# First expert layer (layer 1) computed on tokens sorted by expert: indexed transfers, 40 blocks of 256 rows, weights copied from a register address

## The reference

```python
h = rmsnorm(x, g1); c = h @ w_down
... causal attention with 16 heads of 4 on c ...
x = x + o @ w_up
t = rmsnorm(x, g2).reshape(-1, D)                  # 4096 tokens, D = 128
probs = softmax(t @ router_w)                      # E = 8 experts
vals, idx = top_k(probs, 2);  w = vals / sum(vals)
gate = sum(one_hot(idx, E) * w)                    # two entries per token
hid = silu(einsum('td,edf->tef', t, w1)) * einsum('td,edf->tef', t, w3)   # F = 256
y = einsum('tef,efd->ted', hid, w2)
return res + einsum('ted,te->td', y, gate)
```

## Time and profile before

| | |
|---|---|
| median of three runs | 2375.21 us |
| the profiled execution, its time | 2380.9 us |
| its span, first to last instruction | 2379.1 us |
| mean granted TensorE clock | 0.902 |
| PE busy | 2093.7 us (88%) |
| DVE busy | 1531.5 us (64%) |
| ACT busy | 1066.7 us (45%) |
| POOL busy | 606.8 us (26%) |

### The profile page before, as it was taken

One profiled execution on the slowest core, in us unless ns is written; L12 is line 12 of the kernel. 1 busy time (PEld: TensorE's weight loads), 2 busy tenths in 40 slices (PEclk: granted clock), 3 DMA queues, 4 the chain that ended last, 5 costly groups with the idle time before them and its releaser, 6 DMA issues. The chain is left out here.

```text
span 2379.1 us, 40889 instructions
## 1 busy us (share of the span) xinstructions
PE 2093.7 (88%) x15206; PEld 1293.5 (54%) x15206; DVE 1531.5 (64%) x4178; ACT 1066.7 (45%) x1905; POOL 606.8 (26%) x867
## 2 busy tenths in 40 slices
PE   3688889998588888799999999988899999999993
PEld 1455556676476666455654556544554555555552
DVE  5677665432577776577747766557855677776655
ACT  2344533332355556244543434424354556555542
POOL 3421002001422221232202322243301233433232
PEclk9888889999789999799999999985569999999995
DMA  7556300300455554121200200016520000000001
GB/s 191 108 124 125 65 1 15 57 1 1 82 93 104 105 103 111 36 53 42 57 16 1 45 1 1 1 60 142 128 57 25 10 10 10 9 10 10 10 1 36
DMA packets 153138, 121.94 MB, mean 51 GB/s; under 512 B 21980, under 2 KB 145828, under 8 KB 147236
## 3 DMA queue, kind: packets, MB, share of 16 engines
q1 hardware_dynamic: 152940, 119.32, 23.0%
HBM read 78.04 MB, written 39.85 MB: 50 GB/s over the span
## 5 line engine op out<-in xcount | busy, mean ns | idle before, releaser
L1841 DVE TENSOR_REDUCE mneg<-psb 128x4 f32<-128x512 f32 (+1 forms) x576 | 388.7, 685 | 168.4 <-PE psb L1441 165.8
L2139 ACT ACTIVATE HB<-psb 128x512 f32<-128x512 f32 x384 | 226.7, 598 | 203.7 <-PE psb L1441 200.7
L1441 PE MATMUL psb<-K,Q 96*128 96x128 bf16 x1280 | 192.4, 256 | 54.7 <-DVE mneg L1841 32.7
L1440 PE MATMUL psb<-HB,KS 128*128 128x512 f32 x512 | 232.9, 598 | 0.0
L1441 PE MATMUL psb<-Q,K 99*128 99x128 bf16 x1280 | 150.3, 251 | 79.6 <-DMA Q<-mT 79.4
L1982 DVE TENSOR_TENSOR OE<-psb,OE 128x512 f32<-128x512 f32 x120 | 82.7, 689 | 191.1 <-ACT OE L2211 190.4
L2321 POOL TENSOR_SCALAR rs<-mv 128x2 f32<-128x2 f32 (+1 forms) x104 | 24.0, 230 | 712.0 <-DVE mv L1799 704.0
L2211 ACT ACTIVATE OE<-psb 128x512 f32<-128x512 f32 x128 | 76.5, 597 | 287.6 <-PE psb L1440 287.3
L2139 ACT ACTIVATE HB<-psb,bias 128x512 f32<-128x512 f32 x192 | 131.9, 687 | 145.4 <-PE psb L1441 143.8
L2207 ACT ACTIVATE HB<-psb,cols 128x512 f32<-128x512 f32 x256 | 171.3, 690 | 44.5 <-PE psb L1440 43.2
L1441 PEld LDWEIGHTS psb<-K,Q 96*128 96x128 bf16 x1280 | 112.1, 113 | 132.3 <-issue 61.5
(11 more groups left out here) (347 smaller groups left out, 4637.4 us busy)
## 6 DMA issues: line engine op xcount, KB each, us to landing
K<-sc_k SPq DMA_DIRECT2D x32, 384.0 KB, 5.0
Q<-sc_q SPq DMA_DIRECT2D x32, 384.0 KB
sc_q<-comp SPq DMA_DIRECT2D x48, 192.0 KB, 2.3
sc_q<-comp SPq DMA_DIRECT2D x48, 128.0 KB, 2.1
vraw<-in_ctx SPq DMA_DIRECT2D x48, 128.0 KB, 6.9
KS<-sc_s SPq DMA_DIRECT2D x16, 384.0 KB
K<-sc_k SPq DMA_DIRECT2D x32, 192.0 KB, 3.6
Q<-sc_q SPq DMA_DIRECT2D x32, 192.0 KB, 4.4
```

What stands on the lines that cost most here:

```text
L1440: return pe.e.matmul(out, w, x, start=start, stop=stop)
L1441: return pe.e.matmul(out, w, x, start=start, stop=stop, skip_group_check=True)
L1841: t = e.tensor_reduce(m.mneg[:, s.b % 4, s.i * A.per:(s.i + 1) * A.per], PSB[s.use.bank].rearrange("p (h k) -> p h k", h=A.per), AX.X, ALU ...
L2139: a.done(act(m.HB[:, s.slot, :], PSB[s.use.bank], ACT.Exp, bias=bz), s.use.drained)
```

## The change

The first expert layer no longer sends all tokens through all experts. Each of the 8192 pairs of a token and one of its two experts gets a row of a table in DRAM, sorted by expert; 40 blocks of 256 rows are then computed, each by one expert, and each token fetches its two results.

- All eight fronts (sorted_front) now stand in run_f1, started after every fourth b. gate_rank is followed by gate_pick (12 DVE instructions, for gate_top's 9: masks and weights of the first and second expert) and place: PE counts with small bf16 matmuls how many tokens of each expert stand before each token, and DVE makes row numbers of it (five instructions).
- scatter: POOL writes the normalized tokens to tok_rows by indirect transfers, eight of 128 rows per group, 64 in all. 
- The weights w1 and w3 are split into high and low parts in run_f1 (8 times halves of 128x512), not in the expert stage.
- block_table: after the last front, 24 small DVE instructions write for each block where its rows start and where its expert's weights stand, into an SBUF table. SP writes zero rows behind each expert's last row (pad_rows, 16 transfers, eight of them at an address read from the table).
- expert_blocks: for each of 40 blocks SP loads 256 rows from an address in the table; PE turns them; ACT copies them out of PSUM; DVE splits them; ACT and DVE copy the high and low parts of the expert's weights, 128x512 each, from an address in a register to a fixed buffer; PE computes 12 f32r matmuls of 256 columns and 4 f32 matmuls of 128x128; ACT, DVE: silu and product; DVE copies the result out of PSUM; SP stores it to y_rows. The number of blocks is fixed. Each address is read by the engine itself from the table (value_load): 40 times each on PE, DVE and ACT, 48 times on SP.
- gather and combine: for each b POOL fetches the two result rows of each token (two indirect transfers), and DVE adds them with their weights to U and X. Four b come before the preparations of layer 2's attention, eight among these, and 20 in its main loop, one per b.
- load2, and with it every preparation of layer 2's attention, is now started behind the blocks.

```diff
     def end_f1(b, k, u):
...
-        if b in (3, 7):
-            front1(b // 4, ("vraw", 0), "big_r")
+        if b % 4 == 3:
+            front1(b // 4)
...
+    def expert_blocks(t_m, w_done):
...
+        for n in range(NBLK + 2):
+            if n == 4:
+                do("y_index", need=(tuple(scattered), start), done=t_idx)
+            for j in ([0, 1] if n == 0 else [n + 1]):
+                if j < NBLK:
+                    do("block_load", j=j, need=(ready, start), free=t_full.get(j - 3))
...
+            if n < NBLK:
+                j = n
...
+                do("block_turn", j=j, use=u, need=(loaded[j], start), raw_free=split_done.get(j - 2), free=up_full.get(j - 2), done=split_done[j])
...
+                do("block_weights", j=j, need=(t_tab, t_m, w_done, start), free=up_full.get(j - 2), hi=w_ready[j][0], lo=w_ready[j][1])
+            if 0 <= n - 1 < NBLK:
+                j = n - 1
...
+                do("block_up", j=j, ua=ua, ub=ub, need=(split_done[j], w_ready[j]), at_free=h_done.get(j - 2), h_free=(down_full.get(j - 8), start))
...
+            if 0 <= n - 2 < NBLK:
+                j = n - 2
...
+                do("block_down", j=j, use=u, need=h_done[j], free=stored.get(j - 3))
+                down_full[j] = u.full
+                do("block_store", j=j, need=u.drained)
...
+    chain([(lambda i=i: split_weights(i), 10) for i in range(8)], 10)
     run_f1()
...
-    moe(5, up1, None, each1, lambda g: load2() if g == 0 else None)
...
+    y_stored, blocks_done = expert_blocks(t_m, tuple(w_done))
+    after_blocks = now()
+    for b in range(4):
+        gather(b, y_stored, blocks_done)
+    load2()
+    chain([lambda b=b: gather(b, y_stored, blocks_done) for b in range(4, 12)], 2)
+
+    def more(t):
...
+        if t + 12 < B:
+            gather(t + 12, y_stored, blocks_done)
...
     def block_up(s):                                   (PE)
...
+        for u, at_ in ((s.ua, 0), (s.ub, 256)):
+            pe.wait_ge(u.before)
+            o = PSB[u.bank]
+            for c in range(2):
+                w = slice(at_ + 128 * c, at_ + 128 * c + 128)
+                oc = o[:, 256 * c:256 * c + 256]
+                matmul(oc, m.whi[k][:, w], x[0], c == 0, False, False)
+                matmul(oc, m.whi[k][:, w], x[1], False, False, False)
+                t = matmul(oc, m.wlo[k][:, w], x[0], False, c == 1, False)
...
     def block_weights(s):                              (DVE; the same on ACT with whi and CFr)
+        v.wait_ge(s.need, s.free)
+        at_ = e.value_load(m.tab[0:1, 1, s.j:s.j + 1], min_val=0, max_val=4096 - 512)
+        v.done(e.tensor_copy(m.wlo[s.j % 2], m.WBr[:, bass.ds(at_, 512)]), s.lo)
...
     def gather(s):                                     (POOL)
+        g.wait_ge(s.need, s.free)
+        for k in range(2):
+            e.indirect_dma_start(m.gy[s.k][:, 128 * k:128 * k + 128], None, m.y_rows,
+                                 bass.IndirectOffsetOnAxis(ap=m.pidx[:, k, s.b:s.b + 1], axis=0)).then_inc(g.sems[f"dma_gy{s.k}"], 16)
...
     def block_load(s):                                 (SP; rows_of reads the address)
+        sp.wait_ge(s.need, s.free)
+        load(f"xs{s.j % 3}", m.xs[s.j % 3].rearrange("p (i d) -> p i d", i=2), rows_of(m.tok_rows, (0, s.j)).rearrange("(p i) d -> p i d", i=2))
```

More of the change, by code:

```diff
@@ L1080, in make_plan, with split_weights @@
     do("moe1_load", need=pe_after_ffn0)
-    t_m = dma("dma_moe1", 3)
+    t_m = dma("dma_moe1", 2)
     w_f[0] = now()
+    w_done = []
+    def split_weights(i):
+        w_done[:] = [halves(("CFr", 512 * i), ("WBr", 512 * i), ("WB", 512 * i), t_m, w_f[0])]
+    chain([(lambda i=i: split_weights(i), 10) for i in range(8)], 10)
     run_f1()
[L1084 to L1119, removed]
@@ L1121, in make_plan @@
-    moe(5, up1, None, each1, lambda g: load2() if g == 0 else None)
-    do("moe2_load", need=now())
+    while side:
+        slot_no[0] += 1
+        run_side(1)
+    y_stored, blocks_done = expert_blocks(t_m, tuple(w_done))
[5 more added lines that the diff above has]
+    def more(t):
+        if t == 0:
+            while 11 not in gathered():
+                slot_no[0] += 1
+                run_side(1)
+        if t + 12 < B:
+            gather(t + 12, y_stored, blocks_done)
@@ L1125, in make_plan, with gathered @@
+    def gathered():
+        return [s.b for s in P.steps if s.kind == "gather"]
+    do("moe2_load", need=after_blocks)
     t_w2, t_w1a = dma("dma_w2"), dma("dma_w1a")
-    do("k8_ones", need=P.last["pe"])
+    do("k8_ones", need=after_blocks)
     k8_free[0:4] = [inc("pool", "clear_pool")] * 4
@@ L1609, in gate_rows, with place @@
         pe.done(t, s.use.full)
[L1611 to L1622, removed]
-            pe.done(product(PSB[s.ub.bank], (m.KFr[:, o2:o2 + 128], m.WBr[:, o2:o2 + 128]), x), s.ub.full)
+    def place(s):
+        o = PSB[s.use.bank]
+        o3 = o[:, 0:32].rearrange("p (b e) -> p b e", b=4)
+        pe.wait_ge(s.need, s.use.before)
+        matmul(o[:, 0:32], m.trib[:, :], m.pickb[:, :, :].rearrange("p b e -> p (b e)"), True, False, False)
+        for j in range(3):
+            matmul(o3[:, j + 1:4, :], m.onesq[:, :], m.pickb[:, j:j + 1, :].broadcast_to([128, 3 - j, 8]), False, False, False)
+        for j in range(4):
+            t = matmul(o[:, 32:40], m.onesq[:, :], m.pickb[:, j, :], False, j == 3, False)
+        pe.done(t, s.use.full)
@@ new lines, in block_turn, with block_up @@
+    def block_turn(s):
+        turn(s.use, m.xs[s.j % 3], 2, s.need, C("ident"))
+    def block_up(s):
+        k = s.j % 2
+        x = m.xhi[k], m.xlo[k]
+        pe.wait_ge(s.need)
+        for u, at_ in ((s.ua, 0), (s.ub, 256)):
[7 more added lines that the diff above has]
+                t = matmul(oc, m.wlo[k][:, w], x[0], False, c == 1, False)
+            pe.done(t, u.full)
@@ new lines, in block_down @@
+    def block_down(s):
+        o, h = PSB[s.use.bank], m.HB[:, s.j % 8, :]
+        at_ = pe.e.value_load(m.tab[0:1, 2, s.j:s.j + 1], min_val=0, max_val=2048 - 256)
+        pe.wait_ge(s.need, s.use.before)
+        for i in range(2):
+            for c in range(2):
+                t = matmul(o[:, 128 * i:128 * i + 128], h[:, 256 * c + 128 * i:256 * c + 128 * i + 128],
+                           m.WB[:, bass.ds(at_ + (4096 + 128 * c), 128)], i == 0 and c == 0, c == 1, False)
+        pe.done(t, s.use.full)
```

277 lines of the change are left out of this document (250 added, 27 removed).

## The result

| | before | after |
|---|---|---|
| median of the first runs (five each) | 2375.21 us | 2392.35 us |
| profiled execution, time and span | 2380.9, 2379.1 us | 2381.07, 2379.3 us |
| run_f1, to the last addition to U | 1237 | 1283 |
| from there to the first turn of a block (called the gap) | - | 38 us |
| expert stage; its blocks | 353 us | 140 us |

The ratio of the runs is 1.0056, 95% interval 1.0029 to 1.0084: slower by 0.6%, 17 us between the medians, where 51 were forecast. The stages of the two profiled executions, which this document compares, sum to no difference (-353 + 46 + 38 + 140 + 130, and -1 behind them): that of the changed kernel lies 11 us under its median, that of the kernel before 5.7 over it.

What follows compares the result with a forecast made beforehand. The prediction took PE to bound the 353 us expert stage. It summed -353 + 51 + 45 + 252 + 32 + 24 = +51 onto 2380.9 us, took off 5.7, and forecast 2426 us, range 2395 to 2485 us.

Steps and rivals of the forecast that it cites:

- wrong in the main: The prediction's own test: blocks starting less than 4.8 us apart, or run_f1 not growing.
- forecast 252 us: Expert blocks: 42 x 6.0 us, taking half the blocks at the circle's pace and half at a lower PE clock.
- The circle through SP: Blocks: load of block n+2 waits behind store of n-2; 5.2 plus 5.0 us per two blocks, at least 5.1 each.
- the clock's share of 0.9: Blocks: half run with PE at 1.2 GHz, 6.7 us instead of 5.1, giving near 6.0 us a block.
- my first rival: Blocks: readings cost an instruction's pace, clock holds; about 3.9 us a block, 164 us, 2338 us in all; chance 0.25.
- forecast +32 and +24: Layer 2's attention: +32 us at its start, no longer covered; +24 in its main loop, 1.2 us per b.
- The third rival: Indirect transfers cost POOL the upper bound, 2.1 us, delaying attention and run_f1's splits; 2494 us; chance 0.17.
- forecast +51: run_f1: fronts 2 to 5 31 us, pick and place 10, weight halves 10; 30 to 80 us possible.
- The halves: run_f1: eight splits of 128x512 expert weights into high and low parts on DVE, forecast at 10 us.
- forecast +45: Between run_f1 and the blocks, PE idle: front 7, table instructions, zero-row transfers and the first block's rows.
- Front 7: The last front, starting with the last b and covered by nothing: 18 us (12 to 25) ahead of the blocks.
- my range: The forecast's own range, 2395 to 2485 us: blocks of 5.3 to 6.9 us, the rest 20 us either way.

Runs made afterwards that it cites:

- early_load: Changed kernel with the rows of block n+2 loaded one block earlier, ahead of the store that waits for DVE: 2364.81 us, 0.9932 of the kernel before.
- reads_x5: Changed kernel with each table reading in the blocks on SP and DVE done five times over: 2481.33 us, 1.0433 of the kernel before.
- defer: Changed kernel with each combination two attention steps (in the start two fetches) behind its fetch: 2313.69 us, 0.9706 of the kernel before.
- scatter_apart: Changed kernel with each front's eight indirect stores in four pairs, five slots apart, not one burst: 2380.71 us, 1.001 of the kernel before.
- two edits more: Added to deferral and early loads: new order at the start of layer 2's attention, weight halves behind the block table: 2296.65 us, 0.9648 of the kernel before.

## Why the prediction was wrong

The sign was right, the size was not, and the nearness of the sum is luck: it hides two larger errors that cancel. The forecast named a sign of being wrong in the main, blocks that start less than 4.8 us apart, and they did, at 3.4 in the mean.

- **The blocks: forecast 252 us, measured 140.** This is the step that failed. The circle through SP is there, as forecast: early_load breaks it, and reads_x5 lengthens it by what it adds. Its links were mis-sized. From DVE's copy to PE's turn I had 5.2 us and the trace has 3.2, from the turn to the next copy 5.0 and 3.4. A reading's load takes 0.27 to 0.31 us and the whole reading 0.55 to 0.62, not 1.28 with 0.4 for the registers; I had taken it from a table load on ACT, a different thing. And the sum counted an issue twice: the landing of a load runs from the start of its issue, and PE turns 0.04 us behind it, 2.04 us in all where I had 0.6 + 2.4 + 0.4. I had also let PE's clock fall to 1.2 GHz in half of the blocks, on rows of the start of layer 2's attention, where PE had been idle first; it stayed at 1.00 from 1335 us on. Of the 6.0 us a block, the circle was 1.7 too long and the clock's share of 0.9 did not come. This was my first rival, which gave a block 3.9 us and 164 in all (its own 5.1 - 1.1 is 4.0, a slip of 4 us over the stage): right in its mechanism, and still too slow. The Trainium skill (DMA: Bandwidth & Descriptors, section Latency and other measured facts) gives a floor of about 600 ns; the trace disagrees, since 263 ns is the least of 48.
- **Layer 2's attention: forecast +32 and +24, measured +130.** I had the price of an indirect transfer right (1.2 us taken, 1.25 measured) and saw that DVE would stand if POOL was not ahead, 4.8 us at a time. I then took 1.2 us per b, a quarter of that, by DVE's idle time before. It is the other way round: DVE feeds POOL, so POOL can't be ahead of a DVE that waits. 116 us of waits, 73 of which defer gave back. The start is dearer than forecast too: with the waits gone, defer's stage is still 57 us longer than before, where 32 stood. The third rival named this sign, "DVE's combination waiting for POOL's transfers", with the wrong cause: it needed no dearer transfer. POOL's 64 fetches took 940 to 1124 ns in after, with a median of 956, so what the Trainium skill (SBUF — State Buffer, section SBUF: two separate sides) warns of can have held none of them by more than 0.2 us.
- **run_f1: forecast +51, measured +46.** Right in sum, not in its parts. The halves cost 0 and not 10 us. The bursts of stores, which I had put at nothing, made 19 us of waits for roots, 5 of which scatter_apart took away. What they cost of the 46 us was not run alone. The rest is the fronts' work on DVE, at a little more than its own time. On two chips of the five in the groups there are 30 us more, which no profile of before could tell.
- **The gap: forecast +45, measured 38.** Front 7's 16 us and the table's 7 were forecast as 18 and 5. SP's eight zero rows took 9.5 us where I had 15, since the readings are cheaper.
- **The sum.** With 140 for 252 and 130 for 56 it is -353 + 46 + 38 + 140 + 130 = +1 between the profiled executions, and +17 between the medians. Had I sized only the readings right, I would have forecast the first rival's 2338 us and missed the sign. The lower end of my range does not follow from its own working either: blocks of 5.3 us take 29 us off and the rest 20, which gives 2377 and not 2395. The measured 2392 us would lie inside that, and by luck alone.

## What to carry to other kernels

Before a wait is priced by the idle time of the engine that waits, ask who feeds the engine waited for: where A feeds B, and A then waits for B's next product at once, B is never ahead, and each round costs the whole latency. The remedy was to move the consumer two steps later in the plan, 80 us for a change in order alone. Transfers that an engine issues itself hold up whatever else is queued on it; cutting the bursts into pairs brought 8 us here. And look at the order of the two transfers of a circle before anything in it is made faster: that order alone brought 29 us.

The version to keep has the combinations deferred and the loads a block earlier: 0.9726 to 0.9728 of the kernel before on the chips with stalls. With two edits more, neither of which was worth anything alone, it was 0.9648 (0.9621 to 0.9675) on one without. Both beat both kernels.

## What the runs showed of the hardware

- A reading of a register from a table in SBUF: 0.27 us on SP (least 0.263) and 0.30 on DVE, median; with its register work and check, 0.55 us of SP's queue and 0.62 of DVE's (reads_x5).
- An indirect transfer of 128 rows of 512 bytes: 0.96 us on POOL, the next 1.25 us behind it, whether fetch or store. The rows of a fetch land 2.4 us at least, 2.9 in the median and 6.7 at most behind the start of its issue.
- The granted clock was 1.00 over 125 us of the changed kernel's blocks (PE busy in 98.6) and 0.77 in the mean over 225 us of reads_x5's (busy in 151), a mix of 2.4 and 1.2 GHz. In the attention behind the blocks, where PE had been idle for 30 us first, it was 0.55 over 281 us.
- Chips, or what stands beside them, differ in more than a common factor: on two of five, PE's results come late within bursts of indirect stores and the kernel takes 30 us more, while the kernel before, which has none, takes the same.
